# Inverse edge lengths by square root and reciprocal, and a node phase in four groups

## The chip, the cores and the metric

One core of a Trainium2 chip runs the whole program. The metric is the device time of one execution in microseconds, the median over several executions. Lower is better. The engines are TensorE (PE, its weight loads PEld), VectorE (DVE), ScalarE (ACT), GpSimd (POOL) and SyncE (SP).

## The reference

Four layers of a graph network run one after the other on 6,250 nodes and 100,000 edges. A node row has 64 scalars and 32 three-vectors (160 numbers). A layer gathers node rows over the edges, multiplies them by learned weights and by the direction of the edge, and sums them by node; between two layers the node rows are normalised:

```python
rhat = edge_vec * jax.lax.rsqrt(jnp.sum(jnp.square(edge_vec), -1, keepdims=True) + 1e-12)   # layer 0
rhat = edge_attr / jnp.linalg.norm(edge_attr, axis=-1, keepdims=True)                       # layer 1
...
s = s * jax.lax.rsqrt(jnp.square(s).mean(axis=1, keepdims=True) + EPS) * w0 + b0            # equivariant norm, scalars
v = v * jax.lax.rsqrt(jnp.square(v).mean(axis=(1, 2), keepdims=True) + EPS) * w1[None, :, None]
```

Layers 0 and 1 so need the inverse length of each edge vector, 2 x 100,352 numbers with padding, and each norm needs inverse roots for each node.

## The kernel before

Edges lie as 128 partitions x 784 columns (`ET`), nodes as 56 tiles of 128 rows. The program is a row of stages with a barrier of all engines between them: `setup`, `edge_tables`, `node_phase(None, 0)`, the edges of layer 0, `node_phase(0, 1)`, the edges of layer 1, `node_phase(1, 2)`, the edges of layer 2, `node_phase(2, 3)`, the edges of layer 3 and `node_phase(3, None)`. Below they are called the first (`None, 0`), second (`0, 1`), third, fourth and last phase.

**A node phase** (L2181) makes 7 turns (`PAIRS`) of a loop on every engine. A turn works on two groups of `G` = 4 node tiles (`both`, two objects of class `Group`, L2145, each with its own buffers and half of PSUM). All that is done to a group is a list of stages (`stages`, L2186 on). Each stage belongs to one engine, which waits until the group's semaphore `done` has come to the stage's number (`at`) and raises it at the end. Each engine's program has the stages in order, and in each stage first group 0, then group 1. So one group is a single chain of stages over the engines, and the two groups overlap by one stage. In the second phase a turn is: sums loaded by SP and divided (DVE, L2558 to L2585), turned by PE and moved by ACT, projected (PE, L2315), added to the node rows (DVE, L2589), the norm `ln2_` (DVE, ACT, POOL), two linear layers with gates (PE, ACT, DVE), the sum with the node rows (L2603 to L2614), the norm `end_`, and then the table of layer 1 (PE, ACT), which SP stores. SP's store of a turn waits for the end of the group's list, the loads of the next turn for the stage `turn_a`.

**Roots.** The inverse roots of a norm are taken on POOL by a power of -0.5 (L2294), 128 x 8 for each group: `B.st` holds 4 columns for scalars and 4 for vectors. The `end_` norm needs only the first 4; DVE sets the others to 1.0 (L2715).

**Inverse edge lengths.** `setup` leaves the squared lengths in `W["norm"]` (L299 to L301). In the first phase (for layer 0) and in the second (for layer 1) POOL raises 112 of the 784 columns to the power -0.5 at the end of each turn, behind the roots (L2299). `load_directions` (L569) multiplies the edge vectors by them at the start of the next edge stage.

## Time and profile before

| | |
|---|---|
| median of 3 runs | 13953.59 us (13917.46 to 13966.27) |
| the profiled execution's own time | 13971.56 us |
| its span, first to last instruction | 13969.8 us |
| mean granted TensorE clock | 0.747 |
| busy: PE, DVE, POOL, ACT | 77%, 61%, 59%, 33% |
| the first phase | about 171 to 328 us |
| the second phase | about 3660 to 4229 us |

The profile is of one execution. A timeline row has the start of an instruction from the start of the span, its duration, engine, line and operation, what it writes and reads, its count and, in brackets, the idle time before it with what ended it. SPq is the queue of SP. PEclk is the granted TensorE clock as a share of the full 2.4 GHz, so 0.50 is 1.2 GHz.

### The profile page before, as it was taken

To read this page: it belongs to the slowest core of one execution; us is meant where nothing else is said; L and a number is where in the kernel's file an instruction comes from. 1 tells how busy PE (TensorE), PEld (TensorE's weight loads), DVE (VectorE), ACT (ScalarE), POOL (GpSimd) and SP (SyncE) were. 2 spreads that over 40 slices of the span, in tenths; PEclk is the share of its full clock that TensorE was granted. 3 is DMA by queue.
4 is the path that set the end of the run, shared out by engine and by line. 5 is a ranking of instruction groups with operands and counts; after the bars stand their busy time and mean duration, and the time that the engine had idled before them with its cause. 6 is when DMAs were issued, how large, how long until landed. Compare 5 with 4: busy or idle time off the path is not lost. (4 is left out here: it accounts for less than half of the span.)

```text
span 13969.8 us, 239951 instructions
## 1 busy us (share of the span) xinstructions
PE 10808.1 (77%) x55109; PEld 9201.4 (66%) x55109; DVE 8552.1 (61%) x21245; ACT 4566.3 (33%) x11584; POOL 8205.8 (59%) x8212
## 2 busy tenths in 40 slices
PE   2988888856658999999999457777777656788885
PEld 2888888845556777777777456666666645555564
DVE  4677777789634444444444467777777796566663
ACT  1444444430122222222222235555555501233331
POOL 4777777748625555555655255555555375566660
PEclk7777777768756666666666678888888787788995
DMA  3443444437403333333333322222222274233321
GB/s 91 92 91 91 91 92 92 92 104 207 118 14 65 62 62 63 61 63 61 64 61 61 96 66 67 69 69 69 69 68 68 58 191 128 70 82 82 83 81 45
DMA packets 1350653, 1138.02 MB, mean 81 GB/s; under 512 B 558798, under 2 KB 1147331, under 8 KB 1349895
## 3 DMA queue, kind: packets, MB, share of 16 engines
q0 software_dynamic: 347904, 478.51, 18.0%
q1 hardware_dynamic: 854716, 549.77, 14.3%
q10 hardware_dynamic: 147914, 108.40, 3.0%
q8 instruction: 45, 0.74, 0.0%
q14 instruction: 74, 0.60, 0.0%
HBM read 767.61 MB, written 368.33 MB: 81 GB/s over the span
## 5 line engine op out<-in xcount | busy, mean ns | idle before, releaser
L738 POOL DMA_INDIRECT e_gs<-tab_src,e_ix x1568 | 1680.4, 1072 | 1264.9 <-DVE e_msg L2095 801.6
L677 PE MATMUL e_psF<-w_ident,e_F 128*128 128x128 f32 x6272 | 1395.9, 335 | 756.3 <-ACT e_F L1983 504.7
L738 POOL DMA_INDIRECT e_gd<-tab_dst,e_ix x1568 | 1667.6, 1064 | 477.8 <-issue 473.5
L789 POOL DMA_INDIRECT acc<-e_sums,e_row x784 | 1249.9, 1594 | 1183.5 <-ACT e_sums L1687 1044.4
L677 PEld LDWEIGHTS e_psF<-w_ident,e_F 128*128 128x128 f32 x6272 | 950.8, 180 | 928.6 <-issue 882.3
L707 ACT ACTIVATE e_FT<-e_psF 128x384 f32<-128x384 f32 (+1 forms) x2352 | 1067.6, 454 | 914.2 <-PE e_psF L677 569.4
L1801 POOL DMA_INDIRECT e_g<-tab_src,e_er x976 | 993.3, 1018 | 609.9 <-DVE e_rows L1897 322.0
L1627 PEld LDWEIGHTS e_psS<-e_same,e_rows 128*128 128x128 f32 x6272 | 1129.9, 275 | 313.6 <-issue 310.7
L1627 PE MATMUL e_psS<-e_same,e_rows 128*128 128x128 f32 x6272 | 1248.0, 371 | 1.2 <-DVE e_same L763 1.2
L713 ACT ACTIVATE e_O<-e_psO 128x352 f32<-128x352 f32 (+1 forms) x1568 | 688.1, 439 | 961.7 <-PE e_psO L660 271.7
L1563 PE MATMUL s_psS<-s_wv,s_hot 128*128 128x168 f32 (+1 forms) x3904 | 669.7, 315 | 412.6 <-POOL s_wv L1521 213.7
L738 POOL DMA_INDIRECT e_g<-tab_src,e_ix x784 | 841.8, 1074 | 248.5 <-issue 202.9
L1563 PEld LDWEIGHTS s_psS<-s_wv,s_hot 128*128 128x128 f32 x3904 | 562.6, 191 | 519.4 <-issue 297.1
L1637 PE MATMUL e_psP<-w_l_out_v,e_turned 128*128 128x32 f32 x4704 | 876.4, 334 | 0.0
L1637 PEld LDWEIGHTS e_psP<-w_l_out_v,e_turned 128*128 128x128 f32 x4704 | 872.8, 271 | 0.0
L1682 ACT ACTIVATE e_turned<-e_psS 128x512 f32<-128x512 f32 x784 | 467.4, 596 | 986.6 <-PE e_psS L1627 900.9
L1839 PE MATMUL e_psS<-e_rows,e_hot 128*128 128x384 f32 x1952 | 771.9, 542 | 8.6 <-issue 5.7
L1713 DVE TENSOR_TENSOR e_prod<-e_g,e_dirs 128x384 f32<-128x384 f32 x196 | 109.5, 559 | 1080.7 <-DMA e_g<-tab_src,e_ix 1032.3
L1687 ACT ACTIVATE e_sums<-e_psP 128x192 f32<-128x192 f32 x784 | 258.8, 330 | 1389.5 <-PE e_psP L1637 1168.1
L1635 PE MATMUL e_psP<-w_l_out_s,e_turned 96*128 96x96 f32 x1568 | 419.7, 361 | 310.7 <-ACT e_sums L1687 310.7
L2294 POOL TENSOR_TENSOR n_st<-n_st,w_half 128x8 f32<-128x8 f32 x70 | 113.4, 1637 | 884.6 <-DVE n_st L2718 739.0
L1660 PE MATMUL e_psW<-w_l_fc,e_h 64*128 64x224 f32 x1568 | 619.5, 569 | 1.4 <-ACT e_h L1675 1.4
(492 smaller groups left out, 27261.0 us busy)
## 6 DMA issues: line engine op xcount, KB each, us to landing
val<-e_O SPq DMA_DIRECT2D x392, 320.0 KB
s_val<-val ACTq DMA_DIRECT2D x244, 320.0 KB, 3.3
s_val<-val SPq DMA_DIRECT2D x244, 320.0 KB
e_krow<-in_src_t SPq DMA_DIRECT2D x196, 256.0 KB
sums<-e_total SPq DMA_DIRECT2D x244, 192.0 KB
e_es<-in_es SPq DMA_DIRECT2D x196, 130.0 KB
e_gs<-tab_src,e_ix POOLq DMA_INDIRECT x1568
e_gd<-tab_dst,e_ix POOLq DMA_INDIRECT x1568
```

What stands on the lines that cost most here:

```text
L677: last = nc.tensor.transpose(psF[:, P * g:P * g + P], F[:, k, P * g:P * g + P], ident[:, :])
L707: nc.scalar.activation(FT[:, k, :], psF[:, 0:width], ACT.Copy).then_inc(S.sem(tag + "_FT"), 1)
L713: nc.scalar.activation(O[:, k, :], o[:, 0:width], ACT.Copy).then_inc(S.sem(tag + "_O"), 1)
L738: pool.indirect_dma_start(into[t][u][:, k, :], None, tables[t], bass.IndirectOffsetOnAxis(ix[u][:, t, k:k + 1], 0))\
L789: pool.indirect_dma_start(acc[k], bass.IndirectOffsetOnAxis(T["row"][u][:, k:k + 1], 0), T["sums"][u][:, k, :], None, compute_op=ALU.add). ...
L1563: last = nc.tensor.matmul(psS[u % HALF][:, 0:width], hot[u % HALF][:, k, :], wv[u % HALF][:, k, :], start=(k == 0), stop=(k == TM - 1))
L1627: last = nc.tensor.matmul(psS[:, k % 2, P * c:P * c + P], rows[u][:, k, P * c:P * c + P], T["same"][u][:, k, :], start=True, stop=True, sk ...
L1637: last = nc.tensor.matmul(o[:, 96 + C1 * d:96 + C1 * d + C1], f[:, P * d + P:P * d + 2 * P], W["l1_out_v"][:, :], start=True, stop=True, s ...
L1660: last = nc.tensor.matmul(psWs[u][:, k, 0:wn], h[u][:, P * k:P * k + P], W["l1_fc2"][:, :], start=True, stop=True)
L1682: nc.scalar.activation(turned[k % 2][:, :], psS[:, k % 2, :], ACT.Copy).then_inc(sem("moved"), 1)
L1801: pool.indirect_dma_start(g[u % ROWS4][:, k, :], None, D["tab_src"], bass.IndirectOffsetOnAxis(er[u][:, k, 12:13].bitcast(I32), 0))\
L1839: last = nc.tensor.matmul(psS[u % 2][:, 0:width], hot[u % 2][:, k, :], rows[u % 2][:, k, :], start=(k == 0), stop=(k == TM - 1))
```

## The change

`setup` keeps the squared lengths in new tiles `W["length"]`; ScalarE takes both square roots there, behind its weight loads. POOL's power over the edge lengths goes. In its place DVE does, at the end of each turn of the first and of the second phase, a reciprocal of 112 columns and one Newton step on them (four instructions, each waiting for the one before). The second phase works in four groups of two tiles (`CHAINS` = 4, `G` = 2) in place of two of four; the other phases stay at two of four. The root of the `end_` norm is taken of its own half of `B.st` alone, in all phases, and DVE's fill of the other half goes. The vectors of layer 0 are loaded into the not yet used `logits` tile, not into a tile of their own.

```diff
@@ setup
-    W["half"] = N.sb("half", [P, ET // PAIRS])
+    W["half"] = N.sb("half", [P, 2 * TM])
-    W["norm"] = [N.sb(f"norm{n}", [P, ET]) for n in range(2)]
+    W["norm"], W["length"] = ([N.sb(f"{name}{n}", [P, ET]) for n in range(2)] for name in ("norm", "length"))
...
-            link(nc.vector.tensor_reduce(W["norm"][1][:, :], vec_sq[:, :, :], AX.X, ALU.add))
-            link(nc.vector.tensor_scalar(W["norm"][0][:, :], W["norm"][1][:, :], 1e-12, None, ALU.add))
+            link(nc.vector.tensor_reduce(W["length"][1][:, :], vec_sq[:, :, :], AX.X, ALU.add))
+            link(nc.vector.tensor_scalar(W["length"][0][:, :], W["length"][1][:, :], 1e-12, None, ALU.add))
+            dve.sem_inc(L.sem("lengths"), 1)
...
+            act.wait_ge(L.sem("lengths"), 1)
+            for n in range(2):
+                nc.scalar.activation(W["norm"][n][:, :], W["length"][n][:, :], ACT.Sqrt).then_inc(L.sem("roots"), 1)
@@ load_directions, layer0_edges
-def load_directions(nc, S, D, norm):
+def load_directions(nc, S, D, norm, vec=None):
-    vec, dirs = S.sb("vec", [P, ET, 3]), S.sb("dirs", [P, ET, 5])
+    vec, dirs = S.sb("vec", [P, ET, 3]) if vec is None else vec, S.sb("dirs", [P, ET, 5])
...
+        vec = logits[:, :, :].rearrange("p t h -> p (t h)")[:, 0:3 * ET].rearrange("p (t c) -> p t c", c=3)
+        dirs, sp_dirs, dve_dirs = load_directions(nc, S, D, W["norm"][0], vec)
@@ node_phase
+    G, CHAINS = (2, 4) if post == 0 else (4, 2)
-        both = [Group(S, n, post, pre, n_tab, H) for n in range(2)]
-        X = lambda B, j: W["x"][:, bass.ds((j * 2 + B.n) * G, G), :]
+        both = [Group(S, n, G, post, pre, n_tab, H) for n in range(CHAINS)]
+        newton = S.sb("newton", [P, ET // PAIRS])
+        X = lambda B, j: W["x"][:, bass.ds((j * CHAINS + B.n) * G, G), :]
...
-                            nc.gpsimd.tensor_tensor(B.st[:, :, :], B.st[:, :, :], W["half"][:, 0:2 * G].rearrange("p (a t) -> p a t", a=2), ALU.pow)\
+                            parts = 1 if tag == "end_" else 2
+                            root = B.st[:, 0:parts, :]
+                            nc.gpsimd.tensor_tensor(root, root, W["half"][:, 0:parts * G].rearrange("p (a t) -> p a t", a=parts), ALU.pow)\
                                 .then_inc(B.done, 1)
-                if norms is not None:
-                    share = norms[:, bass.ds(j * (ET // PAIRS), ET // PAIRS)]
-                    nc.gpsimd.tensor_tensor(share, share, W["half"][:, 0:ET // PAIRS], ALU.pow).then_inc(sem("norms"), 1)
...
-                        reduce(B.st[:, 0, :], B.sqr[:, :, :])
-                        nc.vector.memset(B.st[:, 1, :], 1.0).then_inc(B.done, 1)
+                        reduce(B.st[:, 0, :], B.sqr[:, :, :]).then_inc(B.done, 1)
...
+                if norms is not None:
+                    part = bass.ds(j * (ET // PAIRS), ET // PAIRS)
+                    to, square = norms[:, part], W["length"][pre][:, part]
+                    nc.vector.reciprocal(to, to).then_inc(sem("share"), 1)
+                    dve.wait_ge(sem("share"), 4 * j + 1)
+                    tt(newton[:, :], to, to, ALU.mult).then_inc(sem("share"), 1)
+                    dve.wait_ge(sem("share"), 4 * j + 2)
+                    stt(out=newton[:, :], in0=newton[:, :], scalar=-0.5, in1=square, op0=ALU.mult, op1=ALU.mult).then_inc(sem("share"), 1)
+                    dve.wait_ge(sem("share"), 4 * j + 3)
+                    stt(out=to, in0=newton[:, :], scalar=1.5, in1=to, op0=ALU.add, op1=ALU.mult).then_inc(sem("share"), 1)
```

## Rows read from the trace of the kernel before

**Rows 1.** The page, part 1: busy us, share of span, instructions.

```profile
PE 10808.1 (77%) x55109; PEld 9201.4 (66%) x55109; DVE 8552.1 (61%) x21245; ACT 4566.3 (33%) x11584; POOL 8205.8 (59%) x8212
```

**Rows 2.** One line's instructions, L2299: min/median/max ns, first and last start, form.

```profile
L2299 POOL TENSOR_TENSOR w_norm<-w_norm,w_half x14: 18254/18258/18268, 180.5 to 4210.0; 128x112 f32 x14
```

**Rows 3.** Timeline, first phase, first turns: start us, us, engine, line, op, xcount.

```profile
177.25 3.28 POOL L2294 TENSOR_TENSOR nx_st<-nx_st,w_half 128x8 f32<-128x8 f32 x2 [82.56 <-DVE nx_st L2530]
...
198.71 3.24 POOL L2294 TENSOR_TENSOR nx_st<-nx_st,w_half 128x8 f32<-128x8 f32 x2
...
216.03 0.16 DVE L2530 TENSOR_SCALAR nx_st<-nx_st 128x4 f32<-128x4 f32 x1
```

**Rows 4.** Windows, turns 1, 2, 4 of the first phase; columns: engines' busy us (count), PEclk.

```profile
177.25:198.71 21.46, 12.29 (x48) 11.09 (x48) 6.69 (x21) 7.09 (x16) 21.46 (x3) 0.50 0.20 61
198.71:220.14 21.43, 8.39 (x48) 7.40 (x48) 6.64 (x21) 7.09 (x16) 21.43 (x5) 0.66 0.20 61
...
241.56:262.98 21.42, 12.29 (x48) 11.09 (x48) 6.61 (x20) 7.09 (x16) 21.42 (x4) 0.50 0.20 61
```

**Rows 5.** Timeline, end of the first phase.

```profile
309.04 18.27 POOL L2299 TENSOR_TENSOR w_norm<-w_norm,w_half 128x112 f32 x1
...
318.50 0.56 SPq L2260 DMA_DIRECT2D tab_dst<-nx_tab  x1
328.11 0.36 SPq L575 DMA_DIRECT2D e_vec<-in_edge_attr  x1
```

**Rows 6.** DMA, 280 to 330 us: GB/s in 40 slices of 1.25 us.

```profile
GB/s 0 0 0 0 0 0 0 0 0 0 0 0 88 310 296 311 45 0 0 0 0 0 0 0 0 0 0 0 0 134 314 300 298 3 0 0 0 0 0 128
```

**Rows 7.** Timeline, end of the second phase.

```profile
4210.05 18.25 POOL L2299 TENSOR_TENSOR w_norm<-w_norm,w_half 128x112 f32 x1
```

**Rows 8.** DMA, 4218 to 4229 us: GB/s in 40 slices of 0.275 us.

```profile
GB/s 0 0 0 0 0 37 307 319 305 221 2 0 0 0 0 0 0 0 0 123 323 303 317 126 0 0 0 0 0 0 0 0 0 0 0 0 0 0 0 0
```

**Rows 9.** Windows, the last whole turn of the second phase, cut by stage.

```profile
4128.83:4144.97 16.14, 11.39 (x48) 9.83 (x48) 4.28 (x8) 3.67 (x8) 16.14 (x3) 0.50 0.06 20
4144.97:4149.02 4.05, 0.00 (x1) 0.04 (x2) 4.05 (x19) 0.00 (x0) 4.05 (x1) 0.50 0.26 81
4149.02:4160.16 11.14, 10.36 (x48) 9.78 (x48) 1.75 (x4) 2.14 (x4) 1.26 (x1) 0.50 0.00 0
4160.16:4164.25 4.09, 0.00 (x0) 0.00 (x0) 3.53 (x15) 1.55 (x4) 0.00 (x1) 0.50 0.00 0
4164.25:4176.60 12.35, 9.59 (x48) 8.71 (x48) 2.09 (x7) 3.83 (x8) 3.23 (x2) 0.69 0.00 0
4176.60:4182.25 5.65, 0.00 (x0) 0.03 (x1) 1.34 (x5) 5.26 (x20) 0.00 (x0) 0.68 0.00 0
4182.25:4196.60 14.35, 14.18 (x72) 11.72 (x72) 1.99 (x5) 3.11 (x6) 0.00 (x0) 0.74 0.00 0
4196.60:4206.85 10.25, 0.00 (x0) 0.00 (x0) 10.18 (x20) 1.47 (x2) 0.00 (x1) 0.50 0.00 0
```

**Rows 10.** Windows, second phase: the longest turn, and the sum of six.

```profile
3811.16:3895.86 84.70, 52.35 (x216) 46.66 (x216) 29.18 (x77) 21.04 (x52) 24.69 (x5) 0.52 0.06 16
...
sum 473.69, PE 278.57 PEld 245.81 DVE 175.11 ACT 126.03 POOL 148.15; mean PE 46.43 PEld 40.97 DVE 29.19 ACT 21.01 POOL 24.69
```

**Rows 11.** Timeline, setup: the last use of the squared lengths and VectorE's last instruction.

```profile
66.60 0.57 DVE L301 TENSOR_SCALAR w_norm<-w_norm 128x784 f32<-128x784 f32 x1
...
78.02 0.19 DVE L355 COPY w_l_t<-setup_psG 96x32 f32<-96x32 f32 x1 [0.61 <-PE setup_psG L377]
```

**Rows 12.** Timeline, VectorE, phase between layers 2 and 3: reciprocal of 16 columns.

```profile
11913.72 0.37 DVE L2566 RECIPROCAL n_den<-n_den 128x16 f32<-128x16 f32 x2
```

**Rows 13.** Timeline, VectorE: pairs of equal instructions, one for each group.

```profile
4160.16 0.74 DVE L2509 TENSOR_REDUCE n_st<-n_res 128x4 f32<-128x256 f32 x2
...
4198.88 1.56 DVE L2611 TENSOR_TENSOR n_out<-n_out,n_res 128x640 f32<-128x640 f32 x2
```

**Rows 14.** Timeline, last phase: VectorE behind the roots, and the next turn.

```profile
13869.03 0.82 DVE L2724 TENSOR_TENSOR n3x_final<-n3x_cen,n3x_st 128x640 f32<-128x640 f32 x1 [0.68 <-POOL n3x_st L2294]
```

More of the change, by code:

```diff
@@ L243, in setup @@
     whole("l3_w2_v", [96, 32], D["L3_gnn_W2_v"])
-    cleared = [k for k in W if k not in ("x", "na", "ident", "tri", "spare", "half", "norm", "unsorted", "lane", "shift", "keep", "block", "last")]
+    cleared = [k for k in W if k not in ("x", "na", "ident", "tri", "spare", "half", "norm", "length", "unsorted", "lane", "shift", "keep", "block", "last")]
     with ExitStack() as inner:
@@ L805, in layer0_edges @@
         sem = S.sem
-        dirs, sp_dirs, dve_dirs = load_directions(nc, S, D, W["norm"][0])
+        vec = logits[:, :, :].rearrange("p t h -> p (t h)")[:, 0:3 * ET].rearrange("p (t c) -> p t c", c=3)
+        dirs, sp_dirs, dve_dirs = load_directions(nc, S, D, W["norm"][0], vec)
         pair = lambda name, shape: [S.sb(f"{name}{u}", shape) for u in range(2)]
@@ L2145, with __init__ @@
 class Group:
-    def __init__(self, S, n, post, pre, n_tab, H):
+    def __init__(self, S, n, G, post, pre, n_tab, H):
         self.n = n
@@ L2248, in load @@
                     for k in range(TM):
-                        sp.dma_start(B.ag[k][:, :, :], rows(D["acc"][post][k][0:NPAD, :], j * 2 + B.n)).then_inc(B.loaded, 16)
+                        sp.dma_start(B.ag[k][:, :, :], rows(D["acc"][post][k][0:NPAD, :], j * CHAINS + B.n)).then_inc(B.loaded, 16)
                 else:
                     for t in range(G):
-                        slot = sp.value_load(W["last"][0:1, bass.ds((j * 2 + B.n) * G + t, 1)], min_val=0, max_val=V)
+                        slot = sp.value_load(W["last"][0:1, bass.ds((j * CHAINS + B.n) * G + t, 1)], min_val=0, max_val=V)
                         sp.dma_start(B.ag[0][:, t, :], D["sums"][post][bass.ds(slot, 1), :, :].rearrange("o p c -> (o p) c")).then_inc(B.loaded, 16)
@@ L2259, in store @@
                     for n, name in enumerate(("tab_src", "tab_dst")[0:n_tab]):
-                        sp.dma_start(rows(D[name], j * 2 + B.n), B.tab[:, n, :, :]).then_inc(B.stored, 16)
+                        sp.dma_start(rows(D[name], j * CHAINS + B.n), B.tab[:, n, :, :]).then_inc(B.stored, 16)
                 else:
-                    sp.dma_start(rows(D["out"], j * 2 + B.n), B.final[:, :, :]).then_inc(B.stored, 16)
+                    sp.dma_start(rows(D["out"], j * CHAINS + B.n), B.final[:, :, :]).then_inc(B.stored, 16)
             for B in both:
```

4 lines of the change are left out of this document (2 added, 2 removed).

## The prediction

> **What bounds the kernel now.** The page comes first: TensorE is busy 77% of the span, VectorE 61%, GpSimd 59% [rows 1]. The edge stages make these shares, and the change leaves them alone but for one load. So I read the node phases by themselves. The line of the power shows 14 instructions of 18.26 us, 255.6 us in all [rows 2]. Whether they cost time is read from what follows them.
>
> In the first phase they do. A pair of roots starts at 177.25 and the next at 198.71, with no idle time of POOL before it; VectorE has the third pair's input ready at 216.19 [rows 3], yet every turn lasts 21.43 us and POOL is busy in all of it [rows 4]: 18.26 for the power and 3.2 for two roots. At the end of the phase the power starts at 309.04 and ends at 327.31; SP's last store was issued at 318.50, and the next stage begins at 328.11 [rows 5]. The bytes of that store have stopped by 321.3 (slice 33, which has only 3 GB/s left, starts at 321.25) [rows 6].
>
> In the second phase they cost nothing but the tail: the last power runs from 4210.05 to 4228.30 [rows 7], the last bytes are moved by 4224.6 [rows 8]. Before the next norm POOL is long idle: a turn of 78.02 us has 24.7 us of POOL work. That turn, cut by stage, shows alternation: TensorE does nearly all of 16.14 (with the `end_` roots at its start), 11.14 and 14.35 us; VectorE all of 4.05, 4.09 and 10.25 us; ScalarE 5.26 of 5.65 us; and 12.35 us hold the `ln2_` roots and 9.59 us of TensorE [rows 9]. The clock decides too: at a mean grant of 0.52 a turn took 84.70 us, against a mean of 473.69 / 6 = 78.9 [rows 10].
>
> **The change, part by part.**
>
> Setup. The squares are ready at 67.17 and VectorE's last work ends at 78.21 [rows 11], with ScalarE idle between. Two roots of 784 columns, by ScalarE's 0.73 us for 640 columns (1.47 for two, [rows 9]), are 1.8 us; even with a table load in front they end before 78.2. Price nothing; uncovered, 1.8 us. The loaded vectors in another tile, the smaller fill, the dropped fill of 1.0: nothing, they wait for nothing new.
>
> Newton step. Two reciprocals of 16 columns take 0.37 us [rows 12], so 112 columns take at most 7 x 0.19 = 1.3 us. With three instructions of 112 columns at some 0.25 us with their waits (by [rows 13]) the step is at most 2.1 us. Behind them on VectorE is only the next turn's first copy, which waits for the tables: in the 16.14 us stretch VectorE works 4.28 us and is then idle for 7 us [rows 9]; in the first phase it works 6.6 of 21.43 us [rows 4]. Price nothing; uncovered, 2.1 x 14 = 29 us.
>
> First phase. Without the power the turn is VectorE's, TensorE's and ScalarE's chain. From the second roots to the third pair's input it took 216.19 - 198.71 = 17.5 us, in a turn with grant 0.66; in turn 1, at 0.50 throughout, POOL's next input came only just before the power ended, so that chain is about 21.4 us [rows 3, 4]. I take two slow and four fast intervals, as now: 2 x 21.43 + 4 x 17.5 = 112.9 against 128.6, **15.7 us** gained (bounds: none, if all are slow; 23.6, if all are fast). The tail gives 327.31 - 321.3 = **6.0 us**.
>
> Tail of the second phase: 4228.30 - 4224.6 = **3.7 us**.
>
> Price of a smaller instruction. On VectorE two instructions of 640 columns take 1.56 us and two of 256 take 0.74 [rows 13]; with 0.82 and 0.41 for one they start 0.74 and 0.33 apart: 1.07 ns a column and 0.06 fixed, so 320 columns cost 0.40. For the power the only prices are 8 columns in 1.64 (3.28 for two, [rows 3]) and 112 in 18.26 [rows 2]: 0.16 a column and 0.36 fixed, which gives 1.0 us for 4 columns and 0.68 for 2. No row shows fewer than 8; the bounds are 1.64 (price per instruction) and this line.
>
> Four groups, for one turn of the second phase, in the stretches of [rows 9]. (a) 16.14: the first root ends 0.96 earlier and its two VectorE products are 0.68 shorter; TensorE's 11.39 us then run as before, and behind them the last group's move and copy are half: gain 2.0. (b) 4.05, VectorE alone: eight instructions a group become 16 more in all, and the last handover comes later: loss 1.0. (c) 11.14, TensorE: same matmuls, the last addition is half: gain 0.3. (d) 4.09: loss 0.2. (e) 12.35: the first `ln2_` root ends 0.64 earlier and its products are half, but POOL then paces four groups at 0.96: gain 0.6. (f) 5.65, ScalarE: of the last group's activations and the first group's gates half are waited for: gain 1.6. (g) 14.35: gain 0.3. (h) 10.25, VectorE: eight full-width steps with 2 x 0.06 more each, less overlap at the squares: loss 0.7. Sum 2.9, less nothing for TensorE's doubled waits, which its queue takes ahead of time; **7 x 2.9 = 20 us**. Bounds: -4 a turn (rivals 2 and 3 singly) to +5.
>
> The Trainium skill, "VectorE: DVE Perf Modes", section "The TRN2 errata", says that many small tiles each pay a fixed latency and puts the measured fixed part at about 150 cycles, and so speaks against the split. The starts above, 0.74 apart for 640 columns, leave 0.06; by the rule the sum is that of rival 2.
>
> Shorter `end_` root in the other phases, 8 columns to 4, 7 turns each. Third and fourth phase: VectorE's or TensorE's work starts 0.64 earlier, 0.67 x 14 = 9.4. Last phase: the second group's product starts only when the second root is ready (0.68 idle, [rows 14]), so both roots count, 1.25 x 7 = 8.7. **18 us** (bounds 0 and 18).
>
> Sum: 15.7 + 6.0 + 3.7 + 20 + 18 = 63. The profiled execution itself took 13971.56, 18 above the median of 13953.59; taken off the median the forecast is 13890.
>
> **Rivals.**
> 1. *TensorE's clock falls.* Shorter pauses or shorter bursts may leave it at 0.50 in every turn. Then the first phase's 15.7 go, and six turns of the second cost as the slow one, 84.70 against a mean of 78.9: -35. Gain 12, time 13941. For it: two of six intervals of the first phase are at 0.50 [rows 4]. Against: its bursts get denser.
> 2. *Price per VectorE instruction.* If each of the 46 added in stretches b, d and h costs 0.16 us, the whole duration of a 4-column instruction [rows 3], rather than 0.06, a turn is 4.6 worse: gain 63 - 32 = 31, time 13923. Against it: [rows 13].
> 3. *The power costs 1.64 us from 8 columns down.* The 18 go, and with four groups the last of a turn's roots comes 3.3 later, twice: 5.7 a turn worse than reckoned, 40 in all. Gain 5, time 13949.
> 4. *The other side: an instruction on half the columns costs nearly what the whole one did, on POOL and VectorE.* Place: the second phase's four groups. 1.64 a root, and 0.16 for each of the 74 added VectorE instructions (37 a group), 10 a turn more than reckoned: 2.9 - 5.7 - 10 = -12.8 a turn, -90; with 25.4 from the power's removal and none from the roots: 64 slower, 14018. It decides once a turn is longer by over 3.6 us (25.4 / 7).
>
> That the power is off the path anyway is excluded for the first phase by its 21.43 us turns.
>
> **How the numbers follow.** The forecast gets 0.60, rival 1 0.18, rivals 2 and 3 0.08 each, rival 4 0.05, 0.01 left. Its own range is gains of 45 to 90: 24 instead of 15.7 in the first phase, 5 a turn in the second. 0.3%, about what a measurement of this kernel can tell from no change, is 42 us. Faster than that: the forecast and a part of rival 2, 0.64. Within: rivals 1, 3, the rest of 2 and a little of the forecast, 0.30. Slower: rival 4 and a mishap, 0.06. The range goes from 13852 (gain 90 and 12 for the runs' spread) to 13956, above rivals 1 and 3.
>
> **What would show it.** Right: turns of the first phase at 17 to 18 us where the grant is 0.66; the stage after it starting 6 us behind the last table matmuls rather than behind POOL; roots of 4 columns at 1.0 us and of 2 at 0.7; turns of the second phase near 76; edge stages unchanged. Wrong: turns there over 80, POOL roots at 1.6 us, grants of 0.50 through both phases, VectorE's copy waiting behind the Newton step.

## The result, and the profile of the changed kernel

The changed kernel took **13808.28 us** (median of 4 runs, 13802.04 to 13824.12) where the kernel before, run beside it, took 13959.93 (4 runs, 13917.46 to 13992.57): a ratio of 0.9895, 95% interval 0.9866 to 0.9923. That is 152 us faster, where 63 were forecast, and below the low end of the range. The profiled execution of the changed kernel took 13806.19 us, its span 13804.5.

Page, part 1, as [rows 1]: POOL is busy 287 us less, VectorE 52 us more, TensorE 84 us less, though its 55109 matmuls are the same.

```profile
PE 10724.3 (78%) x55109; PEld 9121.1 (66%) x55109; DVE 8604.0 (62%) x21765; ACT 4589.9 (33%) x11782; POOL 7919.1 (57%) x8226
```

The next two tables are windows of the five node phases, from each phase's first instruction to the next stage's: first before, then changed (columns as in [rows 4]). They are shorter by 30.3, 55.3, 14.0, 6.4 and 8.1 us, 114.1 in all.

```profile
170.69:328.29 157.60, 65.85 (x336) 58.39 (x336) 47.25 (x143) 49.63 (x112) 150.06 (x21) 0.61 0.19 58
3660.24:4229.20 568.96, 323.79 (x1512) 285.50 (x1512) 205.27 (x534) 146.97 (x364) 172.88 (x35) 0.58 0.06 17
7761.69:8074.35 312.66, 119.75 (x672) 103.65 (x672) 170.43 (x366) 82.86 (x182) 45.34 (x28) 0.62 0.33 100
11697.72:11950.82 253.10, 135.13 (x672) 118.12 (x672) 113.23 (x254) 51.01 (x98) 22.71 (x14) 0.55 0.13 37
13625.28:13969.18 343.90, 181.70 (x1008) 170.16 (x1008) 124.99 (x408) 57.62 (x112) 22.70 (x14) 0.58 0.16 46
```

```profile
170.34:297.61 127.27, 57.68 (x336) 51.53 (x336) 56.67 (x171) 49.64 (x112) 22.69 (x14) 0.69 0.23 72
3616.69:4130.33 513.64, 300.18 (x1512) 257.21 (x1512) 251.24 (x1068) 172.41 (x560) 48.44 (x56) 0.62 0.06 18
7627.96:7926.63 298.67, 110.96 (x672) 95.59 (x672) 169.63 (x352) 82.76 (x182) 36.58 (x28) 0.65 0.34 105
11536.93:11783.61 246.68, 132.07 (x672) 115.72 (x672) 113.18 (x240) 51.01 (x98) 13.93 (x14) 0.56 0.14 38
13467.81:13803.64 335.83, 182.48 (x1008) 170.79 (x1008) 124.16 (x394) 57.41 (x112) 13.93 (x14) 0.58 0.16 47
```

What the reader is to see is the column of TensorE's busy time beside the granted clock: in the second phase 23.6 us less for the same 1512 matmuls, in the third 8.8 less, at a grant that rose from 0.58 to 0.62 and from 0.62 to 0.65. The forecast moved no clock there.

Turn 1 of the first phase and the sum of its six turns, as [rows 4]. All turns are of the fast kind now (0.69 or 0.70), and POOL works 3.2 us of each.

```profile
176.89:194.65 17.76, 8.70 (x48) 7.81 (x48) 7.95 (x25) 7.09 (x16) 3.28 (x3) 0.69 0.24 74
...
sum 103.78, PE 49.62 PEld 44.35 DVE 47.73 ACT 42.55 POOL 19.45; mean PE 8.27 PEld 7.39 DVE 7.95 ACT 7.09 POOL 3.24
```

A turn of the second phase, cut by stage at the same places as [rows 9] (the eight stretches a to h of the prediction):

```profile
3969.39:3984.25 14.86, 12.15 (x48) 10.04 (x48) 6.24 (x18) 4.58 (x16) 2.98 (x4) 0.50 0.11 33
3984.25:3989.00 4.75, 0.00 (x0) 0.03 (x1) 4.75 (x36) 0.00 (x0) 0.00 (x0) 0.50 0.11 35
3989.00:3997.17 8.17, 7.73 (x48) 7.23 (x48) 2.33 (x7) 2.58 (x8) 0.00 (x0) 0.71 0.22 56
3997.17:4001.26 4.09, 0.00 (x0) 0.00 (x0) 4.07 (x26) 1.92 (x8) 0.00 (x0) 0.50 0.22 57
4001.26:4012.40 11.14, 9.39 (x48) 7.95 (x48) 3.31 (x19) 5.55 (x14) 3.93 (x4) 0.73 0.00 0
4012.40:4016.60 4.20, 0.04 (x1) 0.03 (x1) 1.08 (x7) 3.76 (x16) 0.00 (x0) 0.71 0.00 0
4016.60:4030.90 14.30, 13.87 (x72) 11.77 (x72) 3.78 (x17) 4.62 (x16) 0.00 (x0) 0.74 0.00 0
4030.90:4041.07 10.17, 0.00 (x0) 0.00 (x0) 10.17 (x33) 1.67 (x4) 0.01 (x1) 0.50 0.00 0
```

The third line, stretch c, is the one that differs most: 8.17 us at a grant of 0.71, where [rows 9] have 11.14 at 0.50, with the same 48 matmuls.

POOL's and VectorE's timeline in this turn. Four roots of 2 columns take 2.98 us, four of 4 columns 3.93; the whole Newton step lies between 3973.34 and 3975.20.

```profile
3969.39 2.98 POOL L2303 TENSOR_TENSOR n_st<-n_st,w_half 128x2 f32<-128x2 f32 x4 [35.86 <-DVE n_st L2722]
4001.26 3.93 POOL L2303 TENSOR_TENSOR n_st<-n_st,w_half 128x4 f32<-128x4 f32 x4 [28.90 <-DVE n_st L2535]
```

```profile
3971.73 0.48 DVE L2730 TENSOR_TENSOR n_out<-n_cen,n_st 128x320 f32<-128x320 f32 x1
3972.13 0.48 DVE L2731 TENSOR_TENSOR w_x<-n_cen,n_st 128x320 f32 x1
...
3973.34 0.84 DVE L2743 RECIPROCAL w_norm<-w_norm  x1
3974.22 0.28 DVE L2745 TENSOR_TENSOR n_newton<-w_norm 128x112 f32 x1
...
3974.93 0.27 DVE L2749 SCALAR_TENSOR_TENSOR w_norm<-n_newton,w_norm 128x112 f32 x1
```

In the setup, ScalarE's two roots of 784 columns (its timeline) end at 68.14, ten microseconds before the setup does.

```profile
66.54 1.60 ACT L387 ACTIVATE w_norm<-w_length 128x784 f32<-128x784 f32 x2 [22.01 <-DVEq L302]
```

### The profile page after: what moved, and what is told of

It reads as the page before. It is cut to its first block and busy times, and to the rows that moved or that the text cites. A ratio compares the mean times of both kernels' runs of the same rounds, so it can differ in the third digit from the quotient of the medians.

```text
span 13804.5 us, 240954 instructions
## 1 busy us (share of the span) xinstructions
PE 10724.3 (78%) x55109; PEld 9121.1 (66%) x55109; DVE 8604.0 (62%) x21765; ACT 4589.9 (33%) x11782; POOL 7919.1 (57%) x8226
## 5 line engine op out<-in xcount | busy, mean ns | idle before, releaser
L2303 POOL TENSOR_TENSOR n_st<-n_st,w_half 128x4 f32<-128x4 f32 (+2 forms) x98 | 98.9, 1028 | 936.3 <-DVE n_st L2722 688.2
L1640 PEld LDWEIGHTS e_psP<-w_l_out_s,e_turned 96*128 96x128 f32 x1568 | 326.4, 258 | 450.5 <-issue 448.2
```

The source lines that it names most:

```text
L1640: nc.tensor.matmul(o[:, 0:96], f[0:96, 0:P], W["l1_out_s"][:, :], start=True, stop=True, skip_group_check=True)
```

## The experiments

They ran on five chips, and the chips differ: the kernel before had medians of 11733.65, 13954.65, 11737.35, 14246.00 and 14242.90 us. Between them only the edge stages differ much (8744 us together on the first, 11247 on the fourth); so each ratio is to the runs of before beside it, and the node phases are compared through the profiles. Most variants have one profile each. The tail of a phase is the time behind its last roots of the kind that ends a turn.

**The kernel before, unedited**, as a measure of what scatters.

> The kernel before, unchanged, once more with a profile: it shows how far the stages move with no edit at all. Between the two profiles at hand the node phases gave 114 us and the edge stages 50 us, though nothing in the edge stages was edited. Theory A (the edge stages scatter from execution to execution, and the profile of before fell high): the second phase again about 569 us, but the edge stages of layers 0 and 1 differ from the first profile by tens of us. Theory B (the change itself made the edge stages faster, by where its tiles lie or when they start): the layer 1 edges again at 3530 us and layer 0's at 2679, within 5 us.

Measured: 11741.98 us, ratio 1.0002 (0.9993 to 1.0011). Its node phases take 1626.7 us together, 10 less than in the profile shown first: so much the clock's pattern alone moves them. It ran on another chip than that profile, so it does not decide between the two theories on the edge stages.

**Lengths alone.** The change with two groups of four tiles everywhere and the old `end_` root.

```
-    G, CHAINS = (2, 4) if post == 0 else (4, 2)
+    G, CHAINS = (4, 2)
```

> Only the edge lengths by square root, reciprocal and Newton step; two groups of four tiles and the whole-width end_ root stay. Both theories: first phase 30 us shorter (turns of 17.3 us at a grant of 0.70), second phase shorter by its tail of 4 us and no more. Theory A: edge stages within their scatter of the copy, total gain 34 us. Theory B (the new places of tiles, the vectors in the logits tile): edge stages 50 us faster too, total gain 80 to 90 us.

Measured: 11705.55 us, ratio 0.9983 (0.9973 to 0.9993), 28 us. The first phase went from 157.6 to 126.5 us, all six turns fast (windows, first turn and sum); the second did not gain (565.6 to 568.0 us): its tail is 6 us shorter, but one of its turns took 84.6 us. Its edge stages sum to 8736 us, those of the unedited kernel to 8744: Theory A.

```profile
177.30:194.66 17.36, 8.31 (x48) 7.42 (x48) 7.95 (x25) 7.09 (x16) 3.28 (x3) 0.70 0.24 76
...
sum 102.96, PE 48.81 PEld 43.53 DVE 47.72 ACT 42.57 POOL 19.46; mean PE 8.13 PEld 7.25 DVE 7.95 ACT 7.10 POOL 3.24
```

**Groups alone.** The four groups of two tiles in the second phase, the old lengths and the old root.

```
+    G, CHAINS = (2, 4) if post == 0 else (4, 2)
...
```

> Only the four groups of two tiles in the second phase; the power over the edge lengths stays on GpSimd, its root whole. Theory A and the clock theory (shorter pauses between TensorE's bursts bring its clock up in the projection, where the grant was 0.50): second phase turns of 73 us, at a grant of 0.71 in the projection stretch, phase 45 to 50 us shorter, total gain 45 to 50. Rival (the second phase gained through the removed power as well as the groups): turns of 76 us as I had reckoned, phase 20 us shorter.

Measured: 11686.58 us, ratio 0.9965 (0.9953 to 0.9978), 47 us. The second phase went from 565.6 to 521.4 us, 44 less; the rival's 20 and turns of 76 are out. Windows of its turn 3, of stretch c in it, and the sum of six:

```profile
3690.90:3762.57 71.67, 42.66 (x216) 35.83 (x216) 34.66 (x154) 24.59 (x80) 26.09 (x9) 0.64 0.07 19
...
3711.40:3718.97 7.57, 7.13 (x48) 6.63 (x48) 2.32 (x7) 2.58 (x8) 1.65 (x1) 0.77 0.23 57
...
sum 430.31, PE 256.16 PEld 215.17 DVE 208.01 ACT 147.55 POOL 156.55; mean PE 42.69 PEld 35.86 DVE 34.67 ACT 24.59 POOL 26.09
```

So the high clock in stretch c came with the groups, not with the power's removal. The power of 18.25 us is still there in every turn and costs nothing in it; only the tail is longer (23.1 us instead of 17.6). And the turn is 71.7 us, as in the full change, though its `end_` roots are 1.0 us instead of 0.7 and stretch a takes 15.75 us instead of 14.86: stretch c is 0.60 shorter than in the full change (7.57 against 8.17), so a shorter path of about 1 us added nothing to a turn.

**Root alone.** The kernel before with the `end_` root on 4 columns.

```
-                            nc.gpsimd.tensor_tensor(B.st[:, :, :], B.st[:, :, :], W["half"][:, 0:2 * G]...
+                            parts = 1 if tag == "end_" else 2
+                            root = B.st[:, 0:parts, :]
+                            nc.gpsimd.tensor_tensor(root, root, W["half"][:, 0:parts * G]...
```

> Only the end_ root of its own half, 4 columns in place of 8, with the fill of 1.0 gone, in all phases. By the rows: 1.0 us a root; second, third and fourth phase 4 to 5 us shorter, last one 9, total gain 23. If TensorE's clock answers to the shorter pause, the third phase gives 14 us, as in the changed kernel, and the total 30 or more.

Measured: 11701.74 us, ratio 0.9976 (0.9967 to 0.9985), 32 us. Third phase 308.1 to 299.0, last 342.3 to 332.7, fourth 253.2 to 254.4. In the third phase the turns, 41.4 to 46.4 us before, are all at 41.0 and a grant of 0.67, as in the full change. The fourth did not gain. Below, windows of the third phase, sums of six turns: before in the profile shown first, before on this run's own chip, and the root alone.

```profile
sum 259.04, PE 99.62 PEld 86.40 DVE 145.31 ACT 70.93 POOL 38.82; mean PE 16.60 PEld 14.40 DVE 24.22 ACT 11.82 POOL 6.47
...
sum 254.48, PE 94.30 PEld 81.85 DVE 145.26 ACT 70.83 POOL 38.84; mean PE 15.72 PEld 13.64 DVE 24.21 ACT 11.81 POOL 6.47
```

```profile
6785.30:6826.27 40.97, 15.10 (x96) 13.02 (x96) 24.10 (x51) 11.81 (x26) 5.22 (x4) 0.67 0.36 109
...
sum 245.92, PE 90.69 PEld 78.25 DVE 144.57 ACT 70.82 POOL 31.31; mean PE 15.12 PEld 13.04 DVE 24.09 ACT 11.80 POOL 5.22
```

Against the first a turn is 2.19 us shorter, (259.04 - 245.92) / 6; TensorE's busy time is 1.48 of it, and 0.7 is the root. Against the second it is 1.43 shorter, of which TensorE is 0.60: the root's part stays at 0.7 to 0.8, the clock's part depends on which profile of before it is held against.

**The full change once more**, on another chip than the three parts.

> The changed kernel itself, beside the three parts that ran on this chip (lengths alone -28, groups alone -47, shorter root alone -32 us, sum -107). Theory A (the parts add, and the edge stages, whose code is the same, only scatter by some 15 us each from one execution to the next): 100 to 125 us faster than before, some 11620 us, node phases 110 to 120 us shorter in the profile, edge stages together within 40 us of before with both signs among them. Theory B (the change makes the edge stages shorter too, by its layout of tiles): 150 us faster, with every edge stage shorter than before's by 10 us and more.

Measured: 13824.29 us against 13954.65, ratio 0.9908 (0.9883 to 0.9934), 130 us. The node phases took 1522.1 us, as in the first profile (1522.1). Theory A holds within its interval; the point estimate lies above its range. The medians of the three parts, 28, 47 and 32 us on their chip, sum to 107.

**Four groups in every phase.**

```
-    G, CHAINS = (2, 4) if post == 0 else (4, 2)
+    G, CHAINS = 2, 4
```

> All five node phases in four groups of two. Theory A (a turn is a chain of dependent small instructions, and four groups cover each other's waits in every phase): the third, fourth and last phase lose 2 us a turn or more, 40 us in all against the changed kernel, and the first phase 0.5 us a turn. Theory B (in the short chains the doubled instructions of VectorE, its fixed part, and the second pair of roots on GpSimd cost what the cover gives): the three phases together within 10 us of the changed kernel or up to 30 us longer. TensorE's granted clock in the third phase should stay at 0.65 or above by both.

Measured: 13874.95 us, ratio 0.9940 (0.9916 to 0.9964): 51 us behind the full change. Third, fourth and last phase are 12.8, 15.6 and 29.0 us longer than in the full change beside it: Theory B, and beyond its far end. Windows of the third phase (two turns) and the last (sum):

```profile
7771.35:7812.18 40.83, 16.96 (x96) 12.98 (x96) 27.67 (x102) 14.80 (x52) 6.92 (x9) 0.67 0.35 109
...
7854.99:7900.91 45.92, 22.31 (x96) 17.23 (x96) 27.67 (x102) 15.00 (x52) 6.92 (x8) 0.57 0.32 97
...
sum 302.86, PE 158.58 PEld 148.47 DVE 133.31 ACT 57.15 POOL 16.11; mean PE 26.43 PEld 24.75 DVE 22.22 ACT 9.53 POOL 2.69
```

At the same grant of 0.67 a third-phase turn gains 0.1 to 0.5 us (40.83 here, where the change's turns are 41.0); in half of the turns the grant falls, to 0.57 at worst, so the turns of that phase lose by the clock. In the last phase VectorE's work per turn grew from 17.57 to 22.22 us, and the turn from 45.9 to 302.86 / 6 = 50.5: there the added instructions lie on the path.

**A pause.** The full change, with four VectorE copies that nobody reads ahead of `merged` in the second phase, so that stretch c starts later.

```
+        idle = [S.sb(f"still{n}", [P, 512]) for n in range(4 if post == 0 else 0)]
...
+                    for still in idle:
+                        nc.vector.tensor_copy(still[:, :], W["zeros"][:, :])
                     for B in both:
                         at(dve, "merged", B, j)
```

> The changed kernel with four VectorE copies of 128 x 512 before the stage merged in the second phase, so that TensorE is idle longer before stretch c (its transposes for the projection). Theory A (a longer idle time of TensorE before c makes the granted clock fall, as in before, where 20.2 us of idle were followed by 0.50): the copies take some 2.4 us a turn, c goes from 8.2 us at 0.71 back to 11 us at 0.50, a turn grows by 5 us, the whole by 38 us. Theory B (c's length does not depend on TensorE's idle time): a turn grows by the copies alone, 2.4 us, the whole by 17 us, and c stays at 8.2 us.

Measured: 13846.41 us, ratio 0.9914 (0.9885 to 0.9944). The copies start 0.34 us apart (below, VectorE's timeline: from the first copy to the next instruction 1.34 us). Both theories fall for the six whole turns: they took 429.90 us with the copies, and 429.93 without. (The 20.2 us of idle time in the expectation are the stretches a and b together, in which TensorE was busy 11.39; its idle time ahead of c was 5.42, below.) But the time from the phase's start to its first `end_` roots was 71.1 us, where three profiles of the change have 66.2 to 67.5, and so the phase took 518.6 against 514.8 on the same chip.

```profile
4025.90 1.42 DVE L2590 COPY n_still<-w_zeros 128x512 f32<-128x512 f32 x4
4027.24 0.88 DVE L2593 TENSOR_TENSOR n_nrm<-n_nrm,n_cen 128x128 f32<-128x128 f32 x4
```

```profile
3934.66:4006.71 72.05, 42.20 (x216) 36.07 (x216) 37.06 (x158) 24.60 (x80) 6.92 (x8) 0.64 0.07 19
4006.71:4078.01 71.30, 41.45 (x216) 35.36 (x216) 37.07 (x158) 24.59 (x80) 6.92 (x8) 0.67 0.07 19
...
sum 429.90, PE 250.79 PEld 214.03 DVE 222.42 ACT 147.45 POOL 41.53; mean PE 41.80 PEld 35.67 DVE 37.07 ACT 24.57 POOL 6.92
```

TensorE's busy time fell by 43.15 - 41.80 = 1.35 us a turn, exactly what the path grew by. Its idle time ahead of stretch c was longer, and the grant in the turn higher, not lower. In the timelines of TensorE, c's first transposes in before, in the change and with the pause:

```profile
4149.02 3.59 PE L2308 MATMUL n_psA<-w_ident,n_nrm 128*64 128x128 f32 x16 [5.42 <-DVE n_nrm L2585]
```

```profile
3989.00 3.59 PE L2313 MATMUL n_psA<-w_ident,n_nrm 128*64 128x128 f32 x16 [5.69 <-DVE n_nrm L2590]
```

```profile
4027.66 3.37 PE L2314 MATMUL n_psA<-w_ident,n_nrm 128*64 128x128 f32 x16 [7.03 <-DVE n_nrm L2593]
```

After 5.42 us of idle time c ran at 0.50, after 5.69 at 0.71, and after 7.03 its sixteen transposes took 3.37 us instead of 3.59, so the high level came earlier still. By the Trainium skill, "TensorE: Matmul & The Clock Gate", section "Why this matters for your kernels", idle gaps between bursts are to be avoided because they bring the low clock back; the trace agrees in so far as sixteen transposes take 3.59 us at 0.50 (stretch a) and took 3.59 and 3.37 behind these gaps, but how soon the high clock followed goes the other way in these three, so the gap alone does not decide.

**More transposes.** Sixteen on TensorE ahead of `turn_a` in the second and the fourth phase.

```
+                        at(pe, "share", B, j)
+                        for n in range(16 // CHAINS):
+                            nc.tensor.transpose(B.psA[:, 0:P], ident[:, :], ident[:, :])
```

> The changed kernel with sixteen more TensorE transposes of 128 x 128 a turn, before the stage turn_a of the second and the fourth phase, whose result is overwritten unread. Theory A (work of TensorE in stretch b raises the granted clock of c and d): c is at 0.85 or above instead of 0.71 and 1 us shorter, the fourth phase's turn, now 34.0 us at 0.55, falls by 1 us; the whole 10 to 20 us faster. Theory B (the clock of c is set by what TensorE did in the turn before, and 2 us of transposes change nothing): within 5 us, or slower by the time by which the transposes hold back turn_a, at most 0.5 us a turn.

Measured: 13835.75 us, ratio 0.9912 (0.9885 to 0.9940). Neither theory: the second phase took 528.9 us, 14 longer, with turns of 74.2 to 75.0 and one of 66.79; the fourth took 243.5, 3.4 shorter, which three profiles of the change itself (246.7, 246.9 and 255.7) do not tell from scatter. Windows, second phase:

```profile
3880.80:3955.00 74.20, 49.34 (x232) 42.93 (x232) 35.73 (x154) 24.53 (x80) 6.92 (x8) 0.62 0.07 18
3955.00:4021.79 66.79, 41.92 (x232) 35.92 (x232) 35.74 (x154) 24.31 (x80) 6.92 (x9) 0.70 0.07 20
```

Two neighbouring turns with the same instructions differ by 7.4 us, and TensorE's busy time by 7.4.

**A longer pause**: twelve copies.

```
-        idle = [S.sb(f"still{n}", [P, 512]) for n in range(4 if post == 0 else 0)]
+        idle = [S.sb(f"still{n}", [P, 512]) for n in range(12 if post == 0 else 0)]
```

> As the pause of four copies (0.34 us each, 1.34 us on the path of a turn, after which a turn of the second phase took 71.66 us, as without them), now with twelve copies, 4.1 us on the path of a turn. Theory A (the granted clock makes up for what the path adds, and a turn stays at a length and then goes to the next, as 74.9 us in the run with more transposes): six turns of one length between 74.5 and 75.5 us, at a grant between 0.62 and 0.68, 24 us longer in all than the changed kernel. Theory B (turns add: the four copies were hidden by chance): 75.8 us a turn, and with the grant as it was, 0.62.

Measured: 11668.71 us, ratio 0.9938 (0.9921 to 0.9954). Theory A for the turns: after the first ones all are at 75.10, and the six are 21.3 us longer (451.20 against 429.93) where 24.5 were added. For the whole it was too low: up to the first `end_` roots this run took 79.9 us, over 12 more than the change, and the phase 548.7, some 34 longer where 24 were expected.

```profile
3833.39:3908.49 75.10, 42.51 (x216) 36.33 (x216) 39.82 (x166) 24.61 (x80) 6.92 (x8) 0.64 0.07 18
...
sum 451.20, PE 255.65 PEld 218.56 DVE 238.97 ACT 147.67 POOL 41.49; mean PE 42.61 PEld 36.43 DVE 39.83 ACT 24.61 POOL 6.92
```

**Less work.** The full change without the attention bias in the second phase: `bias` and `merged` only pass the turn on.

```
-                        tt(by_head(B.cen, 0, HS), bcast(W["l0_bias"]...), bcast(B.ratio...), ALU.mult).then_inc(B.done, 1)
+                        dve.sem_inc(B.done, 1)
...
-                        tt(B.nrm[:, :, 0:C0], B.nrm[:, :, 0:C0], B.cen[:, :, 0:C0], ALU.add).then_inc(B.done, 1)
+                        dve.sem_inc(B.done, 1)
```

> The changed kernel without the bias of the attention in the second phase (stages bias and merged leave out eight VectorE instructions, 1.7 us of a turn's path; they only pass the turn on). Theory A (the turn is held at a length by the granted clock): a turn stays at 71.7 us, at a lower grant than 0.62, and the whole within 5 us of the changed kernel. Theory B (the path sets the turn): 70.0 us a turn at 0.62, 12 us less in all. Theory C (the shorter path takes the clock one step further): 68.3 us a turn or less, over 20 us less.

Measured: 11680.54 us, ratio 0.9946 (0.9931 to 0.9962). All three theories fall: with less on the path the second phase took 535.9 us, 22 **longer** than the change's 513.6. Windows of three of its turns and their sum:

```profile
3605.05:3683.39 78.34, 50.59 (x216) 44.11 (x216) 34.13 (x146) 24.71 (x80) 6.91 (x8) 0.54 0.06 17
...
3760.90:3830.87 69.97, 42.22 (x216) 36.36 (x216) 34.12 (x146) 24.49 (x80) 6.92 (x9) 0.65 0.07 19
3830.87:3905.05 74.18, 46.44 (x216) 40.24 (x216) 34.13 (x146) 24.71 (x80) 6.92 (x8) 0.59 0.07 18
...
sum 450.98, PE 284.48 PEld 247.16 DVE 204.79 ACT 147.84 POOL 41.49; mean PE 47.41 PEld 41.19 DVE 34.13 ACT 24.64 POOL 6.92
```

**Still less**: `f2_attr`, the product with the attribute, left out as well.

```
-                        tt(B.out[:, :, :], B.out[:, :, :], bcast(B.attr[:, 0, :], 2, CX), ALU.mult).then_inc(B.done, 1)
+                        dve.sem_inc(B.done, 1)
```

> The changed kernel without the bias (bias, merged) and without the multiplication by the attribute (f2_attr) in the second phase: twelve VectorE instructions less, 1.7 and 1.9 us of a turn's path. Theory A (a turn falls by steps of some 3.4 us, as 71.68 and 75.10 were seen): turns at 68.3 us, the second phase some 24 us shorter than with the change. Theory B (a shorter path loses high clock, as with bias and merged left out, where the turns were 70.0 to 78.4 us): a mean turn over 71.7 us.

Measured: 14074.08 us against 14246.00, ratio 0.9888 (0.9863 to 0.9913). The second phase took 500.7 us, 13 to 14 less than in the profiles of the change, its turns 65.1 to 74.4, mean 70.0. So neither theory is right: the mean did fall, by 1.6 us for 3.6 us of work, but not to a step.

```profile
sum 420.03, PE 261.36 PEld 225.94 DVE 195.53 ACT 147.63 POOL 41.48; mean PE 43.56 PEld 37.66 DVE 32.59 ACT 24.60 POOL 6.91
```

**The pause on two groups.** The kernel before with the four copies, at the same place.

```
+                    for still in idle:
+                        nc.vector.tensor_copy(still[:, :], W["zeros"][:, :])
```

> The kernel before (two groups of four tiles, old root) with the four copies of 0.34 us ahead of merged in the second phase. Theory A (the granted clock makes up for a small change of the path here too): the second phase stays at 566 to 569 us. Theory B (a turn of two groups grows by what is put on its path): 1.34 us a turn, 575 to 578 us. Either way the 7.3 us a turn that four groups give are then read as path or as clock: if a turn goes down to 71.7 us by the pause alone, the groups gave only a better place in the clock's pattern.

Measured: 14253.18 us, ratio 1.0005 (0.9990 to 1.0020), second phase 568.5 us. Theory A again: 1.34 us more path in a turn costs nothing. And this pause does not turn two groups into 71.7 us turns, which speaks against the groups' gain being only a lucky place in the clock's pattern; one pause does not exclude it. Windows, sum of its six turns:

```profile
sum 471.77, PE 268.05 PEld 235.56 DVE 183.07 ACT 126.03 POOL 148.16; mean PE 44.68 PEld 39.26 DVE 30.51 ACT 21.00 POOL 24.69
```

**The layout alone**: the kernel before with the edge vectors in the logits' region and two unused length tiles.

```
+    spaces = [N.sb(f"length{n}", [P, ET]) for n in range(2)]
...
-        dirs, sp_dirs, dve_dirs = load_directions(nc, S, D, W["norm"][0])
+        vec = logits[:, :, :].rearrange("p t h -> p (t h)")[:, 0:3 * ET].rearrange("p (t c) -> p t c", c=3)
+        dirs, sp_dirs, dve_dirs = load_directions(nc, S, D, W["norm"][0], vec)
```

> The kernel before with the change's layout of tiles and nothing else (the edge vectors in a region of the logits, two length tiles that nothing uses): Theory A (the layout costs and gives nothing): ratio 0.999 to 1.001, within 15 us. Theory B (the layout gives the edge stages 15 to 35 us): ratio 0.9975 to 0.999, with the cross convolution below 3515 us on the chip of the first two profiles.

Measured: 11737.94 us, ratio 1.0001 (0.9992 to 1.0010). Theory A: the layout costs and gives nothing, on that chip.

**Two more profiles of the kernel before.**

> The kernel before once more, for its profile: on the chip where the changed kernel and its variants took 2666 to 2705 us for the edges of layer 0, 3498 to 3515 for the cross convolution, 3060 to 3074 for the edges of layer 2 and 1671 to 1684 for the plain convolution. Theory A (edge stages scatter from one execution to the next): they lie within these ranges or within 20 us of them, and the node phases are at 158, 569, 312, 253 and 343 us within 4 us each. Theory B (the change made them shorter): the cross convolution is at 3532 us again, as in the profile shown.

> The kernel before for one more profile. If it takes some 13950 us (the chip of the first two profiles), Theory A (scatter) has its cross convolution within 3498 to 3520 us, as the five profiles with the change there; Theory B (something in the change makes that stage shorter) has it at 3525 us or more. If it takes some 11735 us, it says only how much the stage scatters: 2576 to 2595 us so far.

Measured: 11731.93 and 14250.01 us, so both fell on other chips than the first profile, and the question of their expectations, that chip's edge stages, stays open. Node phases 1632.3 and 1631.1 us. The cross convolution took 2578.9 us in the one, where an earlier profile of the same kernel, on another chip with almost the same median, had 2595.2: 16 us of scatter in one stage. In the other the four edge stages together took 11246.7 us; the kernel before with a pause had 11288.5 there.

**A pause in the last two phases**: three copies ahead of `end_mean`.

```
+                    for still in idle:
+                        nc.vector.tensor_copy(still[:, :], W["zeros"][:, :])
                     for B in both:
                         at(dve, "end_mean", B, j)
```

> The changed kernel with three VectorE copies of 128 x 512 (1.0 us) ahead of end_mean in the fourth and the last phase, whose turns are at two lengths now: 34.0 at a grant of 0.55 or 31.1 at 0.61, and 47.0 at 0.57 or 43.9 at 0.62. Theory A (a millisecond's thousandth of idle path moves the turns into one of the two patterns): all turns of a phase at one length, either the short one (20 and 9 us less) or the long one. Theory B (the path adds): each turn 1.0 us longer, the two phases 14 us longer.

Measured: 14133.39 us, ratio 0.9922 (0.9901 to 0.9944). Last phase: every turn at 47.8 us and 0.57, the long kind (Theory A's worse half) and 0.8 us above it; fourth phase 251.3 us, of 35.1 and 32.2 us turns, that is by Theory B 1.0 us above the old two lengths. No gain.

**The full change a third time, and transposes in the last two phases**, at the start of their turns:

```
+                if post in (2, 3):
+                    for B in both:
+                        at(pe, {2: "share", 3: "pair"}[post], B, j)
+                        for n in range(16 // CHAINS):
+                            nc.tensor.transpose(B.psA[:, 0:P], ident[:, :], ident[:, :])
```

> The changed kernel once more, for its interval and its profile on whichever chip it falls. By the node phases, which were 114 us shorter in both profiles of it so far: 114 us less than before (ratio 0.9903 where before takes 11735 us), with an interval that holds this. If the edge stages gave something on top, the gain is 130 us or more where they are longest (before at 14246 us); if the three parts (28, 47, 32) simply add, it is 107 us.

> The changed kernel with sixteen more transposes of 128 x 128 a turn on TensorE ahead of the first real ones, in the fourth and the last phase only (candidate for a better version). Theory A (they draw high clock into these turns, as the fourth phase's turns of 32.56, 34.91 and 31.39 us with them, against 34.0 and 31.1, had it): fourth phase 243 us, last phase 330 us or less, 5 to 12 us in all, 0.999 of the changed kernel. Theory B (the pattern sets the turns, and which of the two lengths comes cannot be moved by this): both phases within 5 us of 247 and 336 us, in sum no gain.

Measured: 14129.17 and 14109.06 us against 14242.90, ratios 0.9914 (0.9895 to 0.9932) and 0.9915 (0.9895 to 0.9936). The change is 114 us faster there, with node phases of 1526.6 us. The transposes left fourth and last phase at 247.3 and 342.1 us, where the change has 255.7 and 332.2: one shorter, the other longer, no better version by this.

## Why the prediction was wrong, and where it was right

Sizes first. Four profiles of the unedited kernel before have node phases of 1636.2, 1626.7, 1632.3 and 1631.1 us; three of the change have 1522.1, 1522.1 and 1526.6. So the node phases gave 100 to 114 us, wherever it ran, against 63 forecast; with 114 alone the time would be 13840, which is below the range as well. The medians differ by 152, 130 and 114 us. What is over the node phases would be in the edge stages, and that stays open. In the first two profiles they sum to 10958.2 before and 10909.5 with the change. Beside the median of 13954.65 us they sum to 10927.9 with the change, and to 10959.1, 10965.1 and 10961.1 in three variants of it that leave them alone: scatter can make it. Beside 11737.35 two variants of the change have 8731.1 and 8751.1, the kernel before and its variant with the new layout 8724.2 and 8725.5: no gain. Beside 14246.00 the kernel before and its variant with a pause have 11246.7 and 11288.5, two variants of the change 11193.4 and 11244.9: there a gain would fit too. These few profiles a side don't settle it, and up to 38 of the first comparison's 152 us have no cause shown.

One subtraction tells path from clock, roughly: a turn less TensorE's busy time in it, from the sums above and [rows 10]. All are turns of the second phase, mean of six, in us.

| kernel | turn | TensorE busy | rest |
|---|---|---|---|
| before | 78.95 | 46.43 | 32.52 |
| before, pause 1.34 | 78.63 | 44.68 | 33.95 |
| groups alone | 71.72 | 42.69 | 29.03 |
| the change | 71.66 | 43.15 | 28.51 |
| pause 1.34 | 71.65 | 41.80 | 29.85 |
| pause 4.1 | 75.20 | 42.61 | 32.59 |
| 1.7 less | 75.16 | 47.41 | 27.75 |
| 3.6 less | 70.01 | 43.56 | 26.45 |

The rest follows what is put on the path (1.34 gives 1.34, or 1.43 with two groups, 4.1 gives 4.08; what is taken away shows in part, 0.76 of 1.7 and 2.06 of 3.6). The busy time moves by -1.8 to +4.3 us by itself, and in all three pauses it falls while the rest grows. It isn't the clock alone, though: in stretch a, at 0.50 in both, the same 48 matmuls were busy 11.39 us with two groups and 12.15 with four. So between two and four groups the clock gave somewhat more than the difference of the busy times says, and the rest somewhat less. Why the clock changes as it does, no run here shows.

**The step that failed** is "(c) 11.14, TensorE: same matmuls, the last addition is half: gain 0.3", and with it the reckoning of all four-group terms at the clock of [rows 9]. The four groups were priced at 2.9 us a turn. The rest gave 32.52 - 28.51 = 4.0, and TensorE's busy time 46.43 - 43.15 = 3.3 more, by the clock, together 7.3; times seven it is 51 instead of 20. In the single turn stretch c gained 2.97, where 0.3 stood: TensorE's busy time in it fell from 10.36 to 7.73, that is 2.63, at a grant that rose from 0.50 to 0.71, and the 0.34 left is the forecast. The bound of +5 a turn was too narrow for the same reason: it took in no change of the clock for the better. Rival 1 had the clock change, but only downwards.

The other stretches, forecast and measured gain: a 2.0 and 1.28; b -1.0 and -0.70; d -0.2 and 0.0; e 0.6 and 1.21; f 1.6 and 1.45; g 0.3 and 0.05; h -0.7 and 0.08. Without c their forecasts sum to 2.6, their measured gains to 3.4. As a sum they stand, by errors that offset each other in part: a missed by 0.72, and "nothing for TensorE's doubled waits", for which no row stood, did not hold there, where its matmuls took 0.76 us more; h lost nothing, where 0.7 was set down.

**First phase.** "I take two slow and four fast intervals, as now" was the second failed step. All six were fast: 128.58 - 103.78 = 24.8 us instead of 15.7, a little over the bound of 23.6. The other end was real too. Of the eleven profiles that have this phase as the change has it, eight have no slow turn, and three have one or two of 21.3 us, at 0.50 where it was read (more transposes; less work; the pause in the last phases). Those stand at the beginning of the phase, and once a turn is fast the following ones stay so. From the phase's last roots to the next stage it took 22.4 us before and 16.9 now: the tail gave 5.5 us of the 6.0.

**Tail of the second phase**: the stretch behind its last `end_` roots went from 22.4 to 17.6 us, 4.8, of which 3.7 were the power's by the prediction.

**Shorter `end_` root.** The line through two prices held: 1.00 us for 4 columns and 0.70 for 2 were measured, 1.0 and 0.68 were estimated; the third and the fourth root of a turn's four, while VectorE is at its products, take 0.85 and 0.83. In the third phase the rest of a turn fell by (43.17 - 16.60) - (40.99 - 15.11) = 0.69 us, 0.67 was forecast, but TensorE gave 1.49 more, so the phase gained 14.0 instead of 4.7. The last gained 8.1 (8.7), with TensorE's time unchanged: right for the reason given. The fourth gained 6.4 (4.7), and that is luck: its usual turn went from 34.5 to 34.0 us, 0.5 instead of 0.67, and 3.1 of the 6.4 are TensorE's time, with one turn of 31.1 at a grant of 0.61. A second profile of the change has 246.9 us there, the third 255.7 and the root alone 254.4, above the 253.1 to 253.4 of before.

**Hidden terms.** Newton's step took 1.86 us (at most 2.1 forecast) ahead of a wait for the tables, and ScalarE's roots ended ten microseconds ahead of the setup's end: both free. Price per instruction: two products of 320 columns start 3972.13 - 3971.73 = 0.40 us apart, the very 0.40 of the line of 0.06 + 1.07 ns a column, so rival 2 and with it the fixed part that the Trainium skill gives ("VectorE: DVE Perf Modes", section "The TRN2 errata") did not come about between queued instructions; stretch b cost 0.70 of the 1.0 set aside. Rival 3 and the root's part of rival 4 fell with the 0.7 to 0.85 us. (Rival 3's 5.7 a turn is not its own "3.3 later, twice", which is 6.6; the 6 us that this would add to its time change nothing here.) Rival 4's mechanism, that half the columns cost more than half, nevertheless decides in the last phase when it is split too: VectorE's mean instruction went from 17.57 / 57 = 0.308 us to 22.22 / 114 = 0.195, so that its work in a turn grew by 4.65 us, and the phase grew by 29 us.

The account: first phase 30.3 (21.7 forecast), second 55.3 (23.7), third 14.0 (4.7), fourth 6.4 (4.7), last 8.1 (8.7): 114 against 63. Of the 51 missed, 23.6 are TensorE's time in the second phase, 8.8 in the third, 9.1 the slow turns of the first, and some 8 the path of the four groups, 4.0 a turn instead of 2.9.

## What to carry to other kernels

Where bursts of TensorE alternate with other engines' stretches, price a turn as two terms, TensorE's busy time (with both clock levels as its bounds, upwards too) and the rest, and test the rest by a pause: if a turn does not grow by what was added, its length is not the sum of its parts. Small gains on such a path should be judged over a whole phase, on several profiles: here 1.3 us more a turn cost nothing in six settled turns and 4 us at the phase's start, and 1.7 us less cost 3.5 a turn. Splitting into more groups paid in the longest chain, gave nothing in the first phase (126.6 against 126.4 us) and lost in the three last ones: in the last phase because VectorE's added instructions lie on the path, in the turns of the third by the clock; in the fourth it was not told apart.

## What the runs showed of the hardware

- Turns repeat to within some 0.01 us at one length that small changes of the path do not move: 71.7 us in the change, in the groups alone and in the two other profiles of the change (71.67 to 71.69, but for their first two turns), and two turns of 71.30 and 72.05 alternating with the pause; 75.10 with 4.1 us more.
- The granted clock of identical code differs by turn: 66.79 us at 0.70 next to 74.20 at 0.62, with the same instructions.
- A long busy stretch did not by itself bring the high clock: in stretch c of before TensorE was busy 10.36 of 11.14 us and the grant stayed at 0.50; with four groups the same 48 matmuls got 0.71, and 0.77 in the run with the groups alone.
- At one grant, 0.50, the same 48 matmuls in four groups were busy 12.15 us instead of 11.39 in two.
- POOL's power costs 0.36 us and 0.16 us a column, as far down as 2 columns: 0.70, 1.00, 1.64 and 18.26 us for 2, 4, 8 and 112.
- VectorE's reciprocal of 112 columns takes 0.84 us, three times what a product of the same width does (0.28).
